# VectorE's order in the first five attention slots: the third batch's x is normalised and turned in parts

## The reference, cut to what matters

```
x = x + tanh(g_xattn) * attention(layernorm(x), ctx)     # x: 16 batches of 512 rows x 512; ctx: 16 x 77 rows x 512
        q = layernorm(x) Wq^T + bq; k, v = ctx Wk^T + bk, ctx Wv^T + bv; 16 heads of 32 columns
        softmax(q k^T / sqrt(32)) v, then Wo^T + bo
x = x + tanh(g_ffn) * ffn(layernorm(x))
        hidden = x W1 + b1;  a sine of hidden, scaled, is added;  relu;  W2, b2        # 2048 hidden columns
```

## Time and profile before

| | us |
|---|---|
| median of 3 runs | 2129.4 (2129.38 to 2129.72) |
| the profiled execution's own time | 2129.02 |
| its span | 2127.2 |
| TensorE busy in the span | 2101.7 (99%) |
| VectorE busy | 1429.3 (67%) |
| ScalarE busy | 1163.1 (55%) |
| GpSimd busy | 399.5 (19%) |

### The profile page before, as it was taken

How to read it: one execution, slowest core, us unless ns; L and a number is a source line. 1 busy time by engine, 2 the same in 40 slices (tenths; PEclk the granted TensorE clock), 3 DMA queues, 4 the chain that set the end, 5 groups by cost and what they waited for, 6 DMA issues and landing times.

```text
span 2127.2 us, 28743 instructions
## 1 busy us (share of the span) xinstructions
PE 2101.7 (99%) x10251; PEld 1702.3 (80%) x10251; DVE 1429.3 (67%) x2445; ACT 1163.1 (55%) x3453; POOL 399.5 (19%) x324
## 2 busy tenths in 40 slices
PE   8999999999999999999999999999999999999999
PEld 7767777777777678888888888888888888888887
DVE  5688777877786586566665666656666666566654
ACT  3477777777777464444544445444444444544543
POOL 3134344344443211010110110101101011010110
PEclk9999999999999999999999999999999999999999
DMA  7554454445444342231221312312123122231210
GB/s 254 140 130 116 127 119 123 118 118 129 113 118 104 129 124 70 50 80 59 57 63 40 80 60 60 78 47 54 60 60 80 59 40 69 51 80 60 40 40 20
DMA packets 367265, 181.86 MB, mean 85 GB/s; under 512 B 294286, under 2 KB 301682, under 8 KB 367122
## 3 DMA queue, kind: packets, MB, share of 16 engines
q1 hardware_dynamic: 366050, 179.52, 32.9%
q0 software_dynamic: 640, 0.47, 0.1%
q10 hardware_dynamic: 432, 0.04, 0.0%
HBM read 106.34 MB, written 56.85 MB: 77 GB/s over the span
## 4 chain that ended last, share of the span: by engine, by line
PE 64%; DVE 1%; ACT 0%; issue 0%; ACTq 0%; DVEq 0%
PE pair_bank L56 32%; PE m_bank L56 32%; DVE w_split L1490 0%; DVE hidden L1524 0%; DVE turns L1520 0%; DVE sine L1517 0%; ACT relu L1450 0%; ACT hidden L1459 0%; ACT turns L1461 0%; DVE stats L182 0%; DVE relu L1507 0%; DVE x_in L207 0%; ACT sine L1466 0%; DVE residual L1532 0%; DVE mean L192 0%
## 5 line engine op out<-in xcount | busy, mean ns | idle before, releaser
L56 PE MATMUL pair_bank<-w_split,relu 128*128 128x512 f32 x3072 | 738.3, 389 | 3.9 <-DVE relu L1507 3.2
L56 PE MATMUL m_bank<-xT,w_split 128*128 128x512 f32 x3024 | 726.3, 389 | 0.0
L56 PEld LDWEIGHTS pair_bank<-w_split,relu 128*128 128x128 f32 x3072 | 576.1, 188 | 125.3 <-issue 3.6
L56 PEld LDWEIGHTS m_bank<-xT,w_split 128*128 128x128 f32 x3024 | 567.6, 188 | 117.9
L1466 ACT ACTIVATE sine<-turns 128x512 f32<-128x512 f32 x256 | 162.1, 633 | 393.4 <-DVE turns L1520 393.4
L963 ACT ACTIVATE exps<-pair_bank,lowest 128x77 f32<-128x77 f32 x1024 | 318.0, 353 | 62.5 <-DVE lowest L1131 62.5
L1450 ACT ACTIVATE relu<-hidden 128x512 fp32r<-128x512 f32 x256 | 162.5, 635 | 330.4 <-PE m_bank L56 228.7
L1507 DVE SCALAR_TENSOR_TENSOR relu<-hidden,relu 128x512 fp32r<-128x512 f32 x256 | 181.1, 707 | 202.2 <-ACT relu L1450 202.2
L1524 DVE SCALAR_TENSOR_TENSOR hidden<-sine,sine_gain,hidden 128x512 f32<-128x512 f32 x256 | 196.9, 769 | 170.2 <-ACT sine L1466 170.2
L202 POOL TENSOR_TENSOR rstd<-var_eps,minus_half 128x4 f32<-128x4 f32 x32 | 38.3, 1196 | 1166.9 <-DVE var_eps L198 1166.9
L963 ACT ACTIVATION_READ_ACCUMULATOR exps<-pair_bank,lowest 128x1 f32 x1024 | 238.8, 234 | 0.0
(11 more groups left out here) (140 smaller groups left out, 1688.9 us busy)
## 6 DMA issues: line engine op xcount, KB each, us to landing
residual<-in_x_dram SPq DMA_DIRECT2D x64, 256.0 KB, 2.7
x_scratch<-residual SPq DMA_DIRECT2D x64, 256.0 KB, 2.1
x_in<-x_scratch SPq DMA_DIRECT2D x16, 1024.0 KB, 5.5
residual<-x_scratch SPq DMA_DIRECT2D x64, 256.0 KB, 3.3
out_dram<-residual SPq DMA_DIRECT2D x64, 256.0 KB, 2.1
quad_scratch<-x_in SPq DMA_DIRECT2D x60, 256.0 KB, 5.0
x_in<-quad_scratch SPq DMA_DIRECT2D x60, 256.0 KB, 4.4
x_in<-in_x_dram SPq DMA_DIRECT2D x8, 1024.0 KB, 6.0
```

The source lines that it names most:

```text
L56: mm = pe.matmul(out, stationary(s), moving(m), start=first and n == 0, stop=last and n == len(PASSES) - 1)
```

## The change

All of it is in VectorE's list; no instruction is added or removed, and the other engines' lists stay as they are.

- Slot (0,0): `sums` of the third batch of x stood whole, with `statistics`, behind `last_value_sums`. Now tiles 0 and 1 follow the second `peaks`, ahead of the first `inverse` and `queries_lo`; tile 2 follows `queries_lo`.
- Slot (0,1): tile 3 of `sums` and `statistics` follow the second `peaks`. `normalise` of this batch does tiles 0 and 1 alone, in its old place.
- Slot (0,2): `turn_rows` of this batch goes away from both of its places. `x_lo` of the second batch (b = 1) does tiles 0 and 1 in the first of these places and tiles 2 and 3 in its own. `normalise` of tiles 2 and 3 follows.
- Slot (0,3): `turn_rows` of tiles 0 and 1 comes behind the second `inverse`, ahead of `heads_lo`.
- Slot (1,0): `turn_rows` of tiles 2 and 3 comes behind `wo_lo`.

```diff
@@ -1184,6 +1184,11 @@
                         heads_lo(s.pair - 1, 1, *s.earlier_values[1][1:])
                     if s.score:
                         peaks(unit + 2, 1)
+                    if b == 0 and g == 0:
+                        sums(dve, 3, x_rows[0], (0, 1))
+                    if b == 0 and g == 1:
+                        sums(dve, 3, x_rows[0], (3,))
+                        statistics(dve, 3)
                     if not s.odd:
                         if s.pair is not None:
                             for c in range(NC - 1):
@@ -1192,8 +1197,10 @@
                             inverse(unit + 1, 0)
                         if g == 0 and 1 <= b and b + 2 <= B:
                             normalise(dve, b + 3, x_rows[b % 2], range(HALF))
-                        if g == 2 and b + 2 <= B:
+                        if g == 2 and 1 <= b and b + 2 <= B:
                             turn_rows(dve, b + 2, range(HALF))
+                        if b == 0 and g == 2:
+                            x_lo(1, range(HALF))
                         if s.pair is not None:
                             copy_probs(s.pair, NC - 1)
                     else:
@@ -1205,22 +1212,24 @@
                             inverse(unit + 1, 0)
                     if s.queries:
                         queries_lo((g + 1) % G, *s.queries[1:])
+                    if b == 0 and g == 0:
+                        sums(dve, 3, x_rows[0], (2,))
                     if s.fill_values:
                         last_value_sums(*s.fill_values)
                     if s.fill_wo:
                         kt, _, bank, h = s.fill_wo
                         wo_lo(kt, bank, h)
-                    if b == 0 and g == 0:
-                        sums(dve, 3, x_rows[0])
-                        statistics(dve, 3)
                     if b == 0 and g == 1:
-                        normalise(dve, 3, x_rows[0])
+                        normalise(dve, 3, x_rows[0], range(HALF))
                     if b == 0 and g == 2:
-                        x_lo(1, range(NT))
+                        x_lo(1, range(HALF, NT))
+                        normalise(dve, 3, x_rows[0], range(HALF, NT))
+                    if b == 1 and g == 0:
+                        turn_rows(dve, 2, range(HALF, NT))
                     if not s.odd:
                         if g == 0 and 1 <= b and b + 2 <= B:
                             normalise(dve, b + 3, x_rows[b % 2], range(HALF, NT))
-                        if g == 2 and b + 2 <= B:
+                        if g == 2 and 1 <= b and b + 2 <= B:
                             turn_rows(dve, b + 2, range(HALF, NT))
                     if g == 3 and b + 3 <= B:
                         statistics(dve, b + 4)
@@ -1228,6 +1237,8 @@
                         gate_output(*s.output[:3], m_bank[s.output[3]])
                     if s.score:
                         inverse(unit + 2, 1)
+                    if b == 0 and g == 3:
+                        turn_rows(dve, 2, range(HALF))
                     if s.values:
                         heads_lo(s.pair, 0, *s.values[0][1:])
```

## The result

| | before | after |
|---|---|---|
| median, us | 2129.35 (6 runs, 2127.62 to 2129.72) | 2144.76 (6 runs, 2141.86 to 2145.93) |
| ratio | | 1.007, 95% interval 1.006 to 1.008 |
| profiled execution: its own time | 2129.02 | 2141.86 |
| its span | 2127.2 | 2140.0 |

The changed kernel is 15.4 us slower by the medians. The profiled execution is the fastest of the six, so its trace shows less than the usual loss: 12.8 us where the medians have 15.4.

What follows compares the result with a forecast made beforehand. TensorE bounds the kernel (busy 2101.7 of 2127.2 us), so VectorE's order pays only where it stands still. Delay 11.3 plus clock 2.3 is 13.6 on 2129.02: 2142.6, so 2143.0 for the median; range 2138 to 2148.

Steps and rivals of the forecast that it cites:

- The early wait: Slot (0,0): VectorE's statistics wait for the third batch's load until 87.4; scores of slot (0,1) start 2 us later, at 89.55.
- the wait of 2.24: TensorE's wait before the scores at 96.39, slot (0,2), for VectorE's low part of the queries; forecast nearly gone.
- The last turn: Slot (1,0): turns of tiles 2 and 3 start behind wo_lo at 123.4 and end at 124.7, before at 110.76.
- the lead: VectorE, slot (0,2) to wo_lo of slot (1,0): ahead of the old order by 2.4 us; bounds none, or behind by 1.
- The queue: SyncE issues 16 block moves after the last turn, 0.67 each, 10.76 us in all; the residual's first tile only then.
- Two chains: From the last turn to slot (1,1)'s exponentials of unit 11: 16.65 us by SyncE and GpSimd, 16.4 by SyncE and ScalarE.
- The clock: TensorE runs at half clock after its wait of 14 us, costing 2.3 us; bounds 0 and 3.3.
- The first rival: The clock falls early, at the new wait near 87.5: last turn at 128, loss 16.9, 2146.3 us; chance 0.32.
- The rival "faster": The moves' lateness is covered and only the lead at slot (1,0) counts: 2126.9 us, or 2124; chance 0.05.

Runs made afterwards that it cites:

- e6: Kernel before with the third batch's statistics in parts and its load issued ahead of the block moves of batch 1: 2125.55 us, 0.9987.
- e8: Kernel before with the third batch's statistics in parts and nothing else, the load in its old place: 2129.34 us, 0.9994.
- e3: Changed kernel with SyncE's block moves of batch 2 queued behind two residual tiles and the keys of slots (0,3) and (1,0): 2142.68 us, 1.0070.
- e4: Changed kernel with ScalarE's x_hi of batch 2 behind the second exponentials of slot (1,1) and VectorE's x_lo in slot (1,2): 2143.89 us, 1.0074.
- e5: Changed kernel with batch 2's block moves behind residual tiles and keys, its x_hi in slot (1,1) and x_lo in slot (1,2): 2135.94 us, 1.0036.
- e1: Changed kernel with the turns of the third batch back in slot (0,2); statistics in parts and split normalise stay: 2132.14 us, 1.0014.
- e7: Changed kernel with SyncE's load of the third batch ahead of the block moves of batch 1: 2142.09 us, 1.0067.

## Why the prediction was right

Forecast 2143.0 with a range of 2138 to 2148; measured 2144.76. In the profiled execution the delay came out as 12.8 us for a forecast of 13.6, and as 13.3 without the preparation. The mechanism is the forecast one. That its size came so near is in part luck: in the sum of 13.6 one term was 1.4 too large and two were together 1.0 too small (see the clock, below).

- **The early wait.** Forecast: VectorE waits for the load until 87.4, about 4.5 us; scores of slot (0,1) at 89.55 after 2 us. Measured: 4.49 us, until 86.91; 1.89 us, at 88.97. Its return was as forecast, too: the wait of 2.24 became 0.25.
- **The last turn.** Forecast 123.4 for its start; measured 123.64. Counted from the first scores, the lead was 1.6 us instead of 2.4 (43.9 against 45.5 us for what followed wo_lo before, at 125.76). The forecast counted the half of x_lo as moved away from behind queries_lo. It did not count it in its new place, where it took 2.26 us for the 1.25 of the turns; from this comes the wait of 2.36 at 104.91. In e6 and e8, which have the turns there, this wait is 1.33 and 1.34.
- **The queue.** 16 moves in 10.72 for 10.76, the residual issued right behind. The moves of this batch took 10.70 to 10.74 in every kernel that was run. The rows give 0.67 each. The estimate of 0.43 each, from "DMA: Bandwidth & Descriptors" of the Trainium skill, section "Why a DMA increments its semaphore by 16 and not by 1", did not hold here.
- **Two chains.** Forecast 16.65 and 16.4 us from the last turn to the exponentials of unit 11. Measured 17.37 (124.94 to 142.31) over GpSimd, which ScalarE noted as a wait of 1.64, so 15.7 over ScalarE. Of the 0.7 us more over GpSimd most lies in its probabilities: 3.28 for two instead of 2.5 (see below). ScalarE's wait at x_hi was forecast as 13 and measured as 12.66; TensorE's stop as 14 and 15.12. e3, e4 and e5 show that each chain alone keeps nearly all of the loss.
- **The clock.** Forecast 2.3 us after the stop. In the trace the transposes took 1.97 instead of 1.03, the value products 3.23 instead of 2.78; but the wait of 1.17 inside the value products went under in this. Its net is near 0.9: queries_lo ended at 146.23, and with 1.92 for the second part the products would have ended at 148.15 at full clock; they ended at 149.02. This term was too large by 1.4; the chain from the last turn to the end of queries_lo was too small by 0.8 (21.3 for 20.5), and the turn 0.2 late. 11.3 + 0.8 + 0.2 + 0.9 are the 13.2 that the scores of slot (1,2) are late, for 13.6. One of the two costs from which the 2.3 was taken was also read too high: the fall at 28 us cost 1.55 and not 1.8 (the same twelve matmuls took 4.61 there and 3.06 in the changed kernel, rows below).
- **The first rival.** In the changed kernel's profiled execution the clock did not fall at the early wait, but fell after that of 2.36 at 104.91, which the forecast did not have: scores took 3.29 instead of 1.95. In the profiles of e3, e4 and e5, whose programs are the same as the changed one's up to there, it did fall behind the early wait. With e1 (no fall) and e8 (a fall), whose lists are also the same up to there, that makes four falls in six profiles. The forecast gave this rival 0.32; that the changed kernel's own profile was without the fall is chance. e3, at 88.35, and e4's clock by stretch:

```profile
88.35 3.45 PE L56 MATMUL pair_bank<-k_diag,qT 128*128 128x308 f32 x12 [2.20 <-DVE qT L1149]
```

```profile
90.00:92.00 2.00, 2.00 (x10) 2.00 (x9) 1.41 (x3) 0.02 (x1) 1.22 (x1) 0.50 1.09 202
108.00:110.00 2.00, 2.00 (x10) 2.00 (x9) 2.00 (x5) 0.60 (x1) 0.00 (x0) 0.50 0.01 4
```

e4's profiled execution (2145.70) had both falls, the changed kernel's (2141.86) one. The five other runs of the changed kernel lie at 2143.9 to 2145.9. That they had both falls would fit, but their clock by stretch was not recorded. The mean clock of each run was: in e3 it is 0.996 at 2141.84 us and 0.994 at 2145.66, in e4 0.996 at 2141.77 and 0.994 at 2146.82. So the clock has a part in the spread. But e7, without the early wait, spreads nearly as widely, and the preparation varies too, by up to 2.8 us between the traces of this study. How the spread divides between them stays open, and with it the 2.6 us between the loss by the medians and that of the profiled execution.
- **The rival "faster".** It was said to need a last turn no later than about 111 us, ten before its place in the changed order. By the forecast's own 124.7 that is nearly 14. The slip only made this rival look nearer than it was.

## What to carry to other kernels

An instruction that is moved later on an engine with idle time is not priced by its own 1.3 us, but by what it releases: ask which queue waits for it first, how long that queue then issues, and what stands behind it in that queue for others. When two chains of nearly equal length hang on one event, undoing either may show nothing; an experiment must take both. And before work is pulled ahead of a critical step, look up when its data lands: of the two kernels with the statistics alone in parts, only the one whose load was issued ahead of the 16 small moves came out below before (e6; e8 did not, and the intervals of the two overlap).

## What the runs showed of the hardware

- GpSimd's multiplications and VectorE's x_lo, which subtracts one part of xT from another, took longer when they ran at the same time. Two multiplications of 128x616 took 3.28 us beside x_lo, and 2.39 in e4, where x_lo comes later. The four subtractions took 4.59 beside them, and 2.50 in e3, where GpSimd had finished before. In slot (0,2) two subtractions took 2.26 beside one multiplication and 1.28 without.
- After TensorE's stops of 2.0 to 2.8 us the granted clock fell from 2.4 to 1.2 GHz in some cases and not in others. At the scores of slot (0,1) it fell after 1.98 in e5, 2.20 in e3 and 2.43 in e8, and did not after 1.89 in the changed kernel and 2.42 in e1 (twelve scores in 1.95). At the transposes of slot (0,2) a stop of 2.36 was followed by twelve scores in 3.29 in the changed kernel and in 1.97 in e3. The preparation's stop of 2.80 us has both outcomes, too; the kernel before, then the changed one:

```profile
27.80 4.61 PE L56 MATMUL pair_bank<-woT,oT 128*128 128x512 f32 x12 [2.80 <-DVE woT L1013]
```

```profile
28.94 3.06 PE L56 MATMUL pair_bank<-woT,oT 128*128 128x512 f32 x12 [2.80 <-DVE woT L1013]
```

  So the length of a stop alone does not decide it.
- In the stop of 15 us, which began at 128.77, the clock was still 1.00 up to 132 us, and fell within the next stretch. TensorE's work began again at half clock, and ran at full clock from 148 us:

```profile
128.00:132.00 4.00, 0.78 (x4) 0.31 (x2) 0.00 (x0) 0.00 (x0) 0.00 (x0) 1.00 0.66 97
132.00:140.00 8.00, 0.00 (x0) 0.00 (x0) 1.82 (x3) 2.49 (x5) 0.80 (x1) 0.57 0.67 116
...
144.00:146.00 2.00, 2.00 (x12) 1.66 (x16) 0.72 (x2) 2.00 (x12) 1.88 (x2) 0.50 1.07 329
146.00:148.00 2.00, 2.00 (x20) 0.43 (x16) 0.30 (x2) 1.90 (x13) 0.40 (x1) 0.82 0.99 369
148.00:150.00 2.00, 2.00 (x19) 1.16 (x12) 0.83 (x2) 1.20 (x2) 1.79 (x2) 1.00 1.02 390
```
